# A two-layer transformer kernel on one core: the loop over thirteen middle bodies against the same bodies written out

## The reference

```
xn = layernorm(x)                                   # x: [16, 256, 256]
x  = x + attention0(xn) + gated_ffn0(xn)            # 16 heads, causal; 704 hidden, dequantised weights
xn = layernorm(x)
x  = x + latent_attention1(xn) + moe_ffn1(xn)       # 16 heads, latent 64; 32 experts, top 6, and a shared one
```

## Time and profile before

| What | Value |
|---|---|
| Time, median of 3 runs | 2131.82 us (2128.59 to 2132.87) |
| The profiled execution's own time | 2133.93 us |
| Its span, first to last instruction | 2132.2 us |
| PE busy / weight loads busy | 1774.9 us (83%) / 1340.1 us |
| DVE / ACT / POOL busy | 1117.8 / 828.9 / 855.4 us |
| Mean granted TensorE clock | 0.968 |

### The profile page before, as it was taken

One profiled execution on the slowest core, in us unless ns is written; L12 is line 12 of the kernel. 1 busy time (PEld: TensorE's weight loads), 2 busy tenths in 40 slices (PEclk: granted clock), 3 DMA queues, 4 the chain that ended last, 5 costly groups with the idle time before them and its releaser, 6 DMA issues.

```text
span 2132.2 us, 48392 instructions
## 1 busy us (share of the span) xinstructions
PE 1774.9 (83%) x16112; PEld 1340.1 (63%) x16112; DVE 1117.8 (52%) x2564; ACT 828.9 (39%) x1598; POOL 855.4 (40%) x988
## 2 busy tenths in 40 slices
PE   2747888889888888988888888888889888888887
PEld 1424666757666675766667576675757667676766
DVE  3566373655637365563636556373655637365442
ACT  2352425343343534334253433535343343533432
POOL 2003343534344353434435343443535344354445
PEclk7678999999999999999999999999999999999999
DMA  5452322313132132313213131321313132232111
GB/s 114 93 146 63 56 54 59 74 49 81 39 85 54 58 67 58 78 39 85 54 57 74 51 80 39 85 55 52 73 52 84 39 85 55 58 70 56 47 60 35
DMA packets 323775, 139.28 MB, mean 65 GB/s; under 512 B 228048, under 2 KB 309008, under 8 KB 323600
## 3 DMA queue, kind: packets, MB, share of 16 engines
q1 hardware_dynamic: 305168, 86.24, 17.9%
q0 software_dynamic: 18432, 50.36, 8.8%
HBM read 102.12 MB, written 29.88 MB: 62 GB/s over the span
## 4 chain that ended last, share of the span: by engine, by line
issue 33%; PE 28%; POOL 11%; DVE 11%; ACT 7%; SPq 6%; DMA 3%; POOLq 0%; ACTq 0%; DVEq 0%
PE s3r L1324 8%; POOL gs L704 4%; PE s2acc L1321 4%; POOL h2l L713 3%; SPq L494 2%; POOL cb L685 2%; PE s2r L1324 2%; SPq L519 2%; PE s1acc L1427 1%; ACT p L872 1%; PE s2r L1532 1%; ACT p L812 1%; DVE th L1205 1%; PE s2r L1575 1%; PE s1a L1324 1%
## 5 line engine op out<-in xcount | busy, mean ns | idle before, releaser
L704 POOL TENSOR_TENSOR gs<-gs,cb 128x512 f32<-128x512 f32 x192 | 243.8, 1270 | 403.0 <-DVE gs L1210 401.6
L713 POOL TENSOR_TENSOR h2l<-th,h2h 128x512 f16<-128x512 f32 (+1 forms) x224 | 247.1, 1103 | 355.6 <-ACT h2h L903 353.3
L903 ACT CAST h2h<-th 128x512 f16<-128x512 f32 (+1 forms) x224 | 131.7, 588 | 538.0 <-DVE th L1205 485.2
L1324 PE MATMUL s3r<-xe,xg 128*128 128x256 f16 x2304 | 285.7, 274 | 20.8 <-issue 20.8
L1321 PE MATMUL s2acc<-xd,h2h 128*128 128x256 f16 x1536 | 270.4, 278 | 19.3 <-POOL h2l L713 19.3
L1324 PE MATMUL s3r<-xe,xu 128*128 128x256 f16 x2304 | 283.3, 273 | 0.2 <-DVE th L1205 0.2
L1210 DVE SCALAR_TENSOR_TENSOR gs<-th,s3r 128x512 f32<-128x512 f32 (+1 forms) x224 | 144.9, 647 | 240.2 <-ACT th L907 240.0
L1324 PEld LDWEIGHTS s3r<-xe,xg 128*128 128x128 f16 x2304 | 223.9, 98 | 54.6 <-issue 25.0
L685 POOL DMA_DIRECT2D cb<-comb_d x384 | 229.6, 604 | 35.9 <-POOL gs L704 20.1
L1324 PEld LDWEIGHTS s3r<-xe,xu 128*128 128x128 f16 x2304 | 225.3, 98 | 27.3 <-DVE th L1205 0.5
L907 ACT ACTIVATE th<-s3r 128x512 f32<-128x512 f32 (+1 forms) x224 | 126.5, 565 | 274.0 <-PE s3r L1324 270.5
(11 more groups left out here) (279 smaller groups left out, 3125.9 us busy)
## 6 DMA issues: line engine op xcount, KB each, us to landing
cb<-comb_d POOLq DMA_DIRECT2D x128, 192.0 KB, 3.4
part_d<-part SPq DMA_DIRECT2D x32, 512.0 KB, 3.2
cb<-comb_d POOLq DMA_DIRECT2D x128, 128.0 KB, 3.1
stacks<-part_d SPq DMA_DIRECT2D x192, 64.0 KB, 2.3
va<-v_d SPq DMA_DIRECT2D x512, 8.0 KB
cb<-comb_d POOLq DMA_DIRECT2D x128, 64.0 KB, 3.1
land<-part_d SPq DMA_DIRECT2D x96, 64.0 KB, 2.5
part<-part_d SPq DMA_DIRECT2D x96, 64.0 KB, 4.2
```

Of the source, the lines that this page charges most:

```text
L704: g.tensor_tensor(gc2[:, p % 2, :], gs2[:, p % 2, :], cb2[:, 2 * (p % 6):2 * (p % 6) + 2, :].rearrange("p a s -> p (a s)"), ALU.mult).then ...
L713: g.tensor_tensor(h2l[0:m, n % 2, 0:w], th2[0:m, n % 2, 0:w], h2h[0:m, n % 2, 0:w], ALU.subtract).then_inc(sem("h2l_made"), 1)
L903: s.copy(h2h[0:m, n % 2, 0:w], th2[0:m, n % 2, 0:w]).then_inc(sem("h2h_made"), 1)
L1324: ins = nc.tensor.matmul(bk, lhs[i][k], rhs[j][k], start=first, stop=last)
```

## The change

On each of the five engines the `Fori` loop becomes a Python loop, so that the thirteen bodies stand one behind the other in the program, each with `it` as a number. The same edit is made for SP, POOL, ACT, DVE and PE; this is PE's:

```diff
@@ -1697,9 +1693,8 @@
             run(pe2(pe, 0), pe1(pe, 1), None, pe3(pe, 0, first_units), pe0(pe, 2), order="first")
-            with pe.Fori(2, B - 1) as it:
-                run(pe2(pe, Before(it)), pe1(pe, it), pe3(pe, Before(it, 2), last_units), pe3(pe, Before(it), first_units),
-                    pe0(pe, Before(it, -1)))
+            for it in range(2, B - 1):
+                run(pe2(pe, it - 1), pe1(pe, it), pe3(pe, it - 2, last_units), pe3(pe, it - 1, first_units), pe0(pe, it + 1))
             run(pe2(pe, B - 2), pe1(pe, B - 1), pe3(pe, B - 3, last_units), pe3(pe, B - 2, first_units), None, order="late")
```

More of the change, by code:

```diff
@@ L629, in _ @@
             run(sp2(sp, 0), sp1(sp, 1), None, sp3(sp, 0, first_units), sp0(sp, 2), order="first")
-            with sp.Fori(2, B - 1) as it:
-                run(sp2(sp, Before(it)), sp1(sp, it), sp3(sp, Before(it, 2), last_units), sp3(sp, Before(it), first_units),
-                    sp0(sp, Before(it, -1)))
+            for it in range(2, B - 1):
+                run(sp2(sp, it - 1), sp1(sp, it), sp3(sp, it - 2, last_units), sp3(sp, it - 1, first_units), sp0(sp, it + 1))
             run(sp2(sp, B - 2), sp1(sp, B - 1), sp3(sp, B - 3, last_units), sp3(sp, B - 2, first_units), None, order="late")
@@ L751, in _ @@
             run(gp2(gp, 0), gp1(gp, 1), None, gp3(gp, 0, first_units), gp0(gp, 2), order="first")
-            with gp.Fori(2, B - 1) as it:
-                run(gp2(gp, Before(it)), gp1(gp, it), gp3(gp, Before(it, 2), last_units), gp3(gp, Before(it), first_units),
-                    gp0(gp, Before(it, -1)))
+            for it in range(2, B - 1):
+                run(gp2(gp, it - 1), gp1(gp, it), gp3(gp, it - 2, last_units), gp3(gp, it - 1, first_units), gp0(gp, it + 1))
             run(gp2(gp, B - 2), gp1(gp, B - 1), gp3(gp, B - 3, last_units), gp3(gp, B - 2, first_units), None, order="late")
@@ L951, in _ @@
             run(act2(act, 0), act1(act, 1), None, act3(act, 0, first_units), act0(act, 2), order="first")
-            with act.Fori(2, B - 1) as it:
-                run(act2(act, Before(it)), act1(act, it), act3(act, Before(it, 2), last_units), act3(act, Before(it), first_units),
-                    act0(act, Before(it, -1)))
+            for it in range(2, B - 1):
+                run(act2(act, it - 1), act1(act, it), act3(act, it - 2, last_units), act3(act, it - 1, first_units), act0(act, it + 1))
             run(act2(act, B - 2), act1(act, B - 1), act3(act, B - 3, last_units), act3(act, B - 2, first_units), None, order="late")
@@ L1305, in _ @@
             run(dve2(dve, 0), dve1(dve, 1), None, dve3(dve, 0, first_units), dve0(dve, 2), order="first")
-            with dve.Fori(2, B - 1) as it:
-                run(dve2(dve, Before(it)), dve1(dve, it), dve3(dve, Before(it, 2), last_units), dve3(dve, Before(it), first_units),
-                    dve0(dve, Before(it, -1)))
+            for it in range(2, B - 1):
+                run(dve2(dve, it - 1), dve1(dve, it), dve3(dve, it - 2, last_units), dve3(dve, it - 1, first_units), dve0(dve, it + 1))
             run(dve2(dve, B - 2), dve1(dve, B - 1), dve3(dve, B - 3, last_units), dve3(dve, B - 2, first_units), None, order="late")
```

## The result

The changed kernel takes 2097.74 us (median of 4 runs, 2096.6 to 2103.21) against 2132.35 for the kernel before beside it (4 runs, 2128.59 to 2134.11): a ratio of 0.9845, interval 0.9823 to 0.9867. It is faster by 34.6 us. I had said 2116 with a range down to 2104: the direction was right, the gain was twice what I forecast, and the time lies outside the range.

The account below looks back on a forecast made before the run. It took SP's way at the body boundary to end last, about half a microsecond after PE's with its jump stall. Terms 9.6 + 2.7 + 2.2 + 2.6 - 1.0 = 16.1 us off gave 2116 us, 8-in-10 range 2104 to 2127.

Parts of the forecast that it names:

- Instruction fetch: Engines' program fetch: a taken branch outside the fetched window stalls, sequential code is prefetched; PE's 3.6 us agree.
- SP's way to the scores: SP from `comb_d<-ct` through the twelve `stacks` loads: 2.2 us saved before them, 2.6 us in them.
- The clock: PE's short drops to 1.2 GHz: two or three more or fewer move the time by 3 or 4 us.
- The jump on PE: Loop-end branch: its 20.8 us go, but gain only as SP's way shortens; the rest becomes a wait at L1330.
- My own sign of being wrong: Profile after: L1330 waits below 0.5 us and bodies near 122.5 us would mean PE's way was longer.
- SP between the bodies, and ahead: SP at the boundary saves 0.8 us for each of 12 jumps, 9.6 us; ahead of the `land` loads, 2.7 us.
- the way that ends last: Boundary: SP's way, from sixteen `o_d<-th` to `xn<-o_d` landing, ends after PE's by about half a microsecond.
- The turned waits: Waits switching between instruction and the one ahead, 0.06 to 0.07 us each; about 1 us lost through POOL's `h2l`.
- The whole stall comes back: Rival, chance 0.14: PE's way at the boundary is the later one, so its 20.8 us return, giving 2107 us.
- The slower one: Rival, chance 0.07: four engines' 56 new fetch packets each cost a wait like PE's, giving 2150 us.

Follow-up runs that it names:

- u_pe: Kernel before with only PE's loop written out, the other engines keeping theirs: 2105.63 us, ratio 0.9894.
- ph_bad: PE alone written out, 14 instructions added per body, 20 at the start, putting fetch packets near where the loop had them: 2120.91 us, ratio 0.9932.
- ph_good: PE alone written out, 14 instructions added per body, 180 at the start, to put fetch packets outside SP's three bursts: 2116.38 us, ratio 0.9914.
- ph_loop: Kernel before with all loops kept and 120 instructions added at the start of PE's program: 2129.35 us, ratio 0.9978.
- st_delay4: PE alone written out, bodies and start as 180-instruction packet placement, but eight added instructions per body became a PE loop run five times: 2136.59 us, ratio 1.0002.
- u_sp: Kernel before with only SP's loop written out, PE still jumping: 2124.25 us, ratio 0.9958.
- u_mid: Kernel before with DVE, ACT and POOL written out, SP and PE keeping their loops: 2130.16 us, ratio 0.9987.
- ph_best: Changed kernel with 2048-instruction PE bodies and 218 instructions in two places where PE waits for first codes, moving packets earlier: 2122.13 us, ratio 0.9937.

## Why the prediction was wrong, point by point

**The step that failed is "Instruction fetch".** I had read that PE fetches 122 packets in the loop, took them to be no part of the change, and costed them at nothing. Between 262 and 1850 us there are 126 in the kernel before and 103 in u_pe, the difference being mostly those of the jumps; but what counts is that they are not in the same places. Connected with it is "SP's way to the scores": I saw that one issue in the burst was held up "by transfers under way, which no register causes", and took 2.6 us for the twelve loads, at most 6.2. Of the held issue I did not ask what held it and whether the change would move that. PE's wait for these loads fell by 14.5 us in the twelve periods (24.7 to 10.2). The largest bound that I had set for all of this way was 8.4. That the packet's place does this is shown by ph_bad against ph_good.

**The clock** I had put into the ranges with 3 or 4 us either way. It was seven stretches against one, and 13.4 us of PE's busy time (1297.9 to 1284.5). Some of it goes with the packets too: ph_loop, with all its jumps, has two stretches, ph_good one, ph_bad four. But st_delay4 has four with no packet in the twelve loads, and these counts are of one execution each. That a shorter wait for `stacks` is what keeps the clock up is argued from where the stretches begin, and not shown by a run that changes nothing else.

**The jump on PE.** "The rest turns into a wait" was right, and so was its size, 1.4 us; it stands one step ahead of the place that I named, at `kst` instead of `xn`. From the whole of the jumps came 8.3 us, and I had said none. Of these the stall itself explains 1 to 3. The rest may be its packets, of which one at 120 and one at 124 us of a body fall among the sixteen `o_d<-th` and the four `va`. In three bodies of the kernel before, at 510, 1007 and 1507 us, such packets held one issue of each; the two longest waits for `xn` that PE has in the twelve periods, 1.35 and 2.05 us of the 6.4, follow two of these. It was not tried by itself. My own sign of being wrong, waits at L1330 below 0.5 us (they are 3.4 / 12 = 0.3), would have said that PE's way was the longer one; it didn't tell the cases apart, since the wait had moved to `kst`.

**SP between the bodies, and ahead.** 9.6 + 2.7 was too much. SP got its time: 1.6 to 2.5 us from the sixteen to `xn<-o_d` instead of 2.87. But PE waited for `xn` for 6.4 us in all, and more than this can't come back: with SP alone written out that wait is 1.6, and with SP on top of PE 0.2 instead of 5.0, 4.8 us each. I had reckoned with the way that ends last at its full length, when another, over the front's loads and `kst`, ended almost at the same time. The scores' part of SP, 2.2 + 2.6, gave 3.2 (24.7 to 21.5 in u_sp).

**The turned waits** were to lose 1 us. u_mid is 2.8 us faster, inside what can be measured; its wait of PE for `h2l`, where I expected the loss, is 5.5 us instead of 10.8, while that on ACT's `p` (L1553) grew from 25.1 to 26.9 and that on `xn` from 6.4 to 11.8.

**The rivals.** "The whole stall comes back" was the nearest in its number, 2107, and wrong in its mechanism. The slower one, fetch packets that stop the other four engines, did not come: 49 more packets (I had said 56), and no wait that names them.

In one sum, over the twelve periods, before to after: PE busy -13.4, stacks -14.5, "issue" -20.8, kst +15.5, xn -3.0, `stacks<-mt` -0.2, and +5.0 for a wait on POOL's `h1p` (L1384, 0.6 to 5.6) make -31.4, against 31.5 measured. The other waits cancel to within a microsecond, though single ones are as large: `h2l` went from 10.8 to 5.4, and `mx` at L1401 from 1.5 to 6.0. Busy time and waits must make up the periods, so this sum says where the time went and not why.

## What to carry to other kernels

PE's program had its fetch packets at fixed instructions, and in the loop they hit the same transfers in every round: when one DMA issue of a burst takes three times as long as its neighbours in each round, look for a packet of an instruction queue that ends just before it does, before putting it down to "traffic", and ask of any change in program length where the packets will fall. Set a stall off against the waits that follow it on the same engine, here `kst` and `xn` together 1.6 us a body; here only what exceeded them was worth removing. And where several ways end close together, as they did here within half a microsecond, shortening one is worth the distance to the next, not its own length.

## What was not expected of the hardware

- One 16 KB fetch packet of PE, which takes 0.9 to 1.6 us in the kernel before, holds one DMA issue of SP in a burst until it is done (up to 1.8 us instead of 0.32 to 0.39), or makes one part in 32 of two 4 KB loads land 1.3 to 2.0 us late (18.7 us of PE's waiting in 12 bodies in ph_best). The Trainium skill ("Runtime: NRT & Kernel Launch", section Instruction fetch mechanics) calls the cost of crossing a block of 256 instructions mostly hidden. For PE itself that holds here (ph_good, with eight packets a body, has no wait of PE named "issue" in the twelve periods); for SP's transfers it doesn't, and the measurement decides.
- A taken branch of PE takes 0.21 us where its target is 5 instructions back, 3.6 where it is some 2100.
- The same instructions, moved by 160 places, are 15 us apart in 1470 (ph_bad and ph_good, one execution each; 4.5 in the medians of the whole time, of which the start takes 8 back).
- An instruction that holds two reached waits shows as 0.05 us on PE's sequencer, but they follow each other every 0.11 us, and 180 of them at the start, where I thought that PE had time, delayed the third `xn<-o_d` by 8 to 10 us.
